# fc1's first half loaded in two parts around row 0 of x, chunks 0 and 1 computed row by row, and the second half's banks transposed behind each chunk's row 1

## The chip, the core and the metric

One core of a Trainium2 chip runs the kernel. TensorE (PE) multiplies and transposes, ScalarE (ACT), VectorE (DVE) and GpSimd (POOL) work on its results, and SyncE (SP) and ScalarE issue the transfers. The metric is the device time of one execution in microseconds (us).

## The reference

x is 32 rows of 256 tokens with 256 features, all float32. Each row has an index that picks one of 16 experts.

```python
h = gelu(einsum('bnd,hd->bnh', x, fc1_w) + fc1_b)        # fc1_w 1024 x 256, exact GELU
shared = einsum('bnh,sh->bns', h, fc2_w) + fc2_b         # fc2_w 192 x 1024
expert_x = einsum('bnh,bph->bnp', h, experts_w[indices]) + experts_b[indices][:, None, :]
out = x + concatenate([shared, expert_x], axis=-1)       # experts_w 16 x 64 x 1024
```

## The kernel before

The 32 rows of x are 16 blocks of R = 2 rows, 512 tokens each. A block's hidden features are K = 8 chunks of 128. Every float32 operand is split into a high part (rounded to the fast format, made by ScalarE with a copy) and a low part (the difference, made by VectorE or GpSimd), and a product is three matmuls: high-high, high-low, low-high. With D = 2 halves of the 256 features a chunk of fc1 is six matmuls of 512 columns. Blocks 0 and 1 are computed plainly (`conv_chunk`), the other 14 by a scheme with seven products in place of eight, whose weight sums are made while the first two blocks run. Every engine has its program written out by hand; the order of the lines is the order in its queue.

The change touches the first microseconds only.

- SyncE issues row 0 and row 1 of x (L318), waits for row 0 (L320), then issues fc1's second half (L321, in `load_w1`), the fc2 pieces, the experts of block 0 (after the index) and everything later. ScalarE issues the index (L615), fc1's first half (L617) and fc1's bias (L618).
- TensorE makes `WARM` = 12 matmuls on the identity (`warm`, L1052), transposes row 0 and row 1 of x into two banks of `tr_ps`, one bank for each half of the features (`x0_banks`, L1046), transposes fc1's first half from four strips (Q = 4) into the two banks of `acc_ps` (`w1_bank`, L1068), transposes the bias (L1206), computes chunk 0 (`first_chunk`, L1093), transposes fc1's second half into the banks of `tr_ps` once x's parts are made (L1209 to L1211), and goes on with `conv_chunk` 1 to 7 (L1086). Chunks 0 to 3 need only fc1's first half.
- ScalarE makes the high parts: `x0_high` (L461), `w1_high` of the first half (L474), then chunk 0's GELU (`conv_chunk` in its own program, L577), `w1_high` of the second half's two banks, chunk 1's GELU, and the fc2 high parts (`w2_high`, L484) between the next GELUs. `conv_high(0)` (`pair_high`, L565) follows the fourth of them.
- VectorE makes the low parts: `x0_low` (L708), `w1_low` (L721), then fc2's squares, which are 32x32 transposes into the banks of `acc_ps` (`w2_square`, L744), and their low parts (`w2_low`, L752). A square of a bank waits for the low part that frees it.
- GpSimd's first work after the identity is the low part of pair 0 of the hidden values (`pair_lo(0)`, L395), which waits for `conv_high(0)`.
- TensorE's first fc2 products (`fc2_first(0, 0, 8)`, L1222, matmuls at L1136) follow chunk 7 and wait for that low part. `conv_chunk(8)`, block 1's first chunk, waits for block 1's low part (`x1_low`, L813).

The order of the second half around chunks 0 and 1 is in ScalarE's program:

```python
conv_chunk(0)
w1_high(1, 0)
w1_high(1, 1)
conv_chunk(1)
w2_high(0)
```

Of the kernel before, what the change touches and what calls it, by code (L numbers as in the profile page):

```python
# [15 lines left out]
def cond_mlp_residual(nc, x, index, fc1_w, fc1_b, fc2_w, fc2_b, experts_w, experts_b, out):  # L16
# [17 lines left out]
    BANK = 512  # L34
    GELUS = 4
    SLOTS = 6
    WARM = 12

# [28 lines left out]
    with ctx:  # L67
# [6 lines left out]
        def sem(name):  # L74
            return ctx.enter_context(nc.semaphore(name))
# [46 lines left out]
        e_loaded = [sem(f"e_loaded{n}") for n in range(2)]  # L122
        be_loaded = [sem(f"be_loaded{n}") for n in range(2)]
        stored = [sem(f"stored{n}") for n in range(2)]
        w1_loaded = [sem(f"w1_loaded{n}") for n in range(2)]
        w1p_loaded = sem("w1p_loaded")
        w2_loaded = sem("w2_loaded")
        b1_loaded = sem("b1_loaded")
# [132 lines left out]
        def feature_chunk(rows, d):  # L261
            return rows.rearrange("p (c d) -> p d c", d=D)[:, d, :]
# [1 line left out]
        def bank(i):  # L264
            return fc1_ps[:, i, :].rearrange("p (j t) -> p j t", j=2)

        def load_w1(queue, half):
            queue.dma_start(w1_in[:, half * HALF:(half + 1) * HALF, :], w1_halves[half])\
                .then_inc(w1_loaded[half], 16)

        block = ctx.enter_context(nc.Block())

# [1 line left out]
        def _(sp):  # L274
# [41 lines left out]
            for b in range(R):  # L316
                ts = slice(b * T, (b + 1) * T)
                sp.dma_start(resid[:, 0, ts, :], x_blocks[0][:, ts, :]).then_inc(x0_loaded[b], 16)  # L318

            sp.wait_ge(x0_loaded[0], 16)  # L320
            load_w1(sp, 1)  # L321
            for q in range(Q):
                sp.dma_start(w2_piece[S * q:S * (q + 1), :, :], w2_v[q]).then_inc(w2_loaded, 16)
            sp.wait_ge(index_loaded, 16)
# [46 lines left out]
        def _(pool):  # L371
            def residual(n, b):
                par = n % 2
                if n == 0:
                    pool.wait_ge(x0_loaded[b], 16)

                    pool.wait_ge(x0_tr, D)
                else:
                    pool.wait_ge(x_loaded[par], 16 * ((n + 1) // 2))
                pool.wait_ge(b2_loaded, 16)  # L380
                pool.wait_ge(be_loaded[par], 16 * R * (n // 2 + 1))
                rows = resid[:, par, b * T:(b + 1) * T, :]
# [73 lines left out]

        @block.scalar
        def _(act):
            def x0_high(d):
                act.wait_ge(x0_tr, d + 1)  # L460
                nc.scalar.activation(xt0[:, d, HI, :], tr_ps[:, d, :], ACT.Copy)\  # L461
                    .then_inc(x0_hi, 1)

            def w1_slots(half, d, v):

# [130 lines left out]
            def lower_pair(t):  # L596
# [15 lines left out]
                act.wait_ge(c21_gelu, 2 * t + 2)  # L612
                pair_high(q)

            act.dma_start(index_sb[:, :], index.rearrange("(o n) -> o n", o=1))\  # L615
                .then_inc(index_loaded, 16)
            load_w1(act, 0)  # L617
            act.dma_start(b1_in[:, :].rearrange("k (q c) -> k q c", q=Q),  # L618
                          fc1_b.rearrange("(q k c) -> k q c", q=Q, c=S))\
                .then_inc(b1_loaded, 16)  # L620
# [2 lines left out]
            nc.scalar.activation(gelu[:, 0, 0, 0:1], ident[:, 0:1], ACT.Gelu)\  # L623
                .then_inc(gelu_loaded, 1)
            act.wait_ge(gelu_loaded, 1)
            for d in range(D):
                x0_high(d)
            for d in range(D):
                w1_high(0, d)
            act.wait_ge(b1_ready, 1)  # L630
            conv_chunk(0)
            w1_high(1, 0)
            w1_high(1, 1)
            conv_chunk(1)
            w2_high(0)
            w2_high(1)
            conv_chunk(2)
# [65 lines left out]

        @block.vector
        def _(dve):
            def x0_low(d):
                dve.wait_ge(x0_hi, d + 1)
                nc.vector.tensor_tensor(xt0[:, d, LO, :], tr_ps[:, d, :],  # L708
                                        xt0[:, d, HI, :].bitcast(FP32), ALU.subtract)\
                    .then_inc(x0_lo, 1)  # L710

            def w1_slots(half, d, v):
                cols = slice(2 * half * P, (2 * half + 2) * P)
# [215 lines left out]
                        else:  # L929
                            nc.vector.tensor_tensor(dst, src, dst, ALU.add).then_inc(drained, 1)  # L930

            for d in range(D):
                x0_low(d)
            for d in range(D):
                w1_low(0, d)
            dve.wait_ge(b1_tr, 1)
            nc.vector.tensor_copy(b1[:, :], fc1_ps[:, 3, 0:K]).then_inc(b1_ready, 1)
            for d in range(D):
# [104 lines left out]
        def _(pe):  # L1043
            def transposes(dst, tiles):
                for c, tile in enumerate(tiles):
                    last = nc.tensor.transpose(dst[:, c * P:(c + 1) * P], tile, ident[:, :])  # L1046
                return last
# [6 lines left out]

            def x0_banks(b):
                pe.wait_ge(x0_loaded[b], 16)
                for d in range(D):
                    last = transposes(tr_ps[:, d, b * SEQ:(b + 1) * SEQ],
                                      [feature_chunk(resid[:, 0, b * T + t, :], d)
                                       for t in range(T)])  # L1060
                    if b == R - 1:
                        last.then_inc(x0_tr, 1)

            def w1_bank(half, d):

                dst = (acc_ps, tr_ps)[half][:, d, :].rearrange("p (k q c) -> p q k c", q=Q, c=S)
                for q in range(Q):
                    last = nc.tensor.transpose(  # L1068
                        dst[:, q], feature_chunk(w1_in[:, half * HALF + q, :], d), ident[:, :])
                last.then_inc(w1_tr, 1)  # L1070

            def conv_operand(j, d, v):

# [14 lines left out]
                                            start=(at == 0), stop=(at == len(terms) - 1))  # L1088
                last.then_inc(conv_filled, 1)

            def first_chunk():
                def product(d, w, v):
                    return nc.tensor.matmul(fc1_ps[:, 0, :], conv_operand(0, d, w), xt0[:, d, v, :],  # L1093
                                            start=(d == 0 and w == v), stop=(d == D - 1 and w == LO))
                for d in range(D):
                    pe.wait_ge(w1_hi, d + 1)
                    product(d, HI, HI)
                    pe.wait_ge(x0_lo, d + 1)
                    product(d, HI, LO)
                for d in range(D):  # L1100
                    pe.wait_ge(w1_lo, d + 1)
                    last = product(d, LO, HI)
                last.then_inc(conv_filled, 1)

            def product(n, g, dst, w, o, fresh):

# [90 lines left out]

            pe.wait_ge(ident_ready, 1)
            warm(WARM)
            for b in range(R):  # L1200
                x0_banks(b)
            pe.wait_ge(w1_loaded[0], 16)
            for d in range(D):
                w1_bank(0, d)
            pe.wait_ge(b1_loaded, 16)
            nc.tensor.transpose(fc1_ps[:, 3, 0:K], b1_in[:, :], ident[0:K, 0:K]).then_inc(b1_tr, 1)  # L1206
            first_chunk()
            pe.wait_ge(w1_loaded[1], 16)
            for d in range(D):  # L1209
                pe.wait_ge(x0_lo, d + 1)  # L1210
                w1_bank(1, d)  # L1211
            conv_chunk(1)
            conv_chunk(2)
            conv_chunk(3)
            pe.wait_ge(w1_lo, 4)
# [102 lines left out]
```

## Time and profile before

| | |
|---|---|
| median of three executions | 357.48 us (357.47 to 357.76) |
| the profiled execution | 357.54 us, its span 355.4 us |
| busy in the span | TensorE 350.9 us, VectorE 259.5, ScalarE 246.8, GpSimd 235.0 |
| transferred | 28.68 MB read from memory, 8.39 MB written |

Times in the rows are us from the span's start. PE is TensorE's matmuls, PEld its weight loads, which run ahead of the matmuls. A row of the timeline merges instructions of one kind that follow each other: start, us, engine, line, operation, output and inputs, shape, count. In square brackets stands how long the engine sat idle before and what it waited for. The "us" of a merged row includes the tail of its last instruction, so that rows of TensorE overlap a little. In the chain of work that ended last the pieces don't overlap.

### The profile page before, as it was taken

The numbers are of one execution on the slowest core, as the hardware profiler recorded it, in microseconds if no ns is written. First come the engines' busy times: TensorE is split into PE (matmuls) and PEld (weight loads), VectorE is DVE, ScalarE is ACT, GpSimd is POOL, SyncE is SP. The second block draws the span as 40 slices with busy tenths as digits, with TensorE's granted clock in tenths as the row PEclk, the third lists the DMA queues.
The fourth block names the chain that finished last, engine by engine and source line by source line (L and its number), as shares of the span: only waits on it lengthen the run. The fifth ranks groups of instructions, "written<-read, shape, count | busy, mean of one in ns | idle before, by whom it ended". The sixth has DMA issues, their size and how long they took to land.

```text
span 355.4 us, 7075 instructions
## 1 busy us (share of the span) xinstructions
PE 350.9 (99%) x2381; PEld 323.7 (91%) x2381; DVE 259.5 (73%) x498; ACT 246.8 (69%) x410; POOL 235.0 (66%) x150
## 2 busy tenths in 40 slices
PE   8999999999999999999999999999999999999996
PEld 5899899999999999999999999999999999999996
DVE  2797976968859697786968869697786968844642
ACT  4885957777678577767777678577777777666560
POOL 0179887658866586865758866576865758855471
PEclk9999999999999999999999999999999999999999
DMA  8779663533333334341533324353332230312001
GB/s 239 172 162 191 140 181 85 148 99 89 112 87 117 89 90 141 94 110 59 149 98 89 114 79 122 90 137 101 84 107 64 90 99 30 120 38 89 31 30 61
DMA packets 69981, 37.53 MB, mean 106 GB/s; under 512 B 43450, under 2 KB 69946, under 8 KB 69946
## 3 DMA queue, kind: packets, MB, share of 16 engines
q1 hardware_dynamic: 69376, 36.55, 38.1%
q10 hardware_dynamic: 570, 0.53, 0.4%
q8 instruction: 19, 0.31, 0.4%
q14 instruction: 16, 0.13, 0.1%
HBM read 28.68 MB, written 8.39 MB: 104 GB/s over the span
## 4 chain that ended last, share of the span: by engine, by line
PE 98%; ACT 0%; issue 0%; POOL 0%; DVE 0%; POOLq 0%; ACTq 0%
PE fc_ps L1110 40%; PE acc_ps L1166 29%; PE acc_ps L1169 15%; PE fc_ps L1086 6%; PE acc_ps L1136 3%; PE acc_ps L1189 2%; PE fc_ps L1166 1%; PE fc_ps L1052 1%; PE fc_ps L1093 1%; PE fc_ps L1169 1%; PE tr_ps L1046 0%; ACT xt L461 0%; PE tr_ps L1068 0%; ACT w1t L474 0%; DVE resid L906 0%
## 5 line engine op out<-in xcount | busy, mean ns | idle before, releaser
L395 POOL TENSOR_TENSOR ht<-gelu,ht 128x1024 fp32r<-128x1024 f32 x62 | 149.5, 2411 | 97.4 <-ACT ht L565 97.4
L1166 PE MATMUL acc_ps<-w2t,ht 128*128 128x512 f32 x448 | 162.4, 397 | 0.0
L1110 PE MATMUL fc_ps<-xt,w1t 128*128 128x256 f32 x1176 | 159.9, 284 | 0.0
L1110 PEld LDWEIGHTS fc_ps<-xt,w1t 128*128 128x128 f32 x1176 | 148.7, 189 | 5.5
L1169 PE MATMUL acc_ps<-w2t,ht 128*128 128x256 f32 x448 | 125.9, 281 | 0.0
L1166 PEld LDWEIGHTS acc_ps<-w2t,ht 128*128 128x128 f32 x448 | 84.4, 188 | 14.9
L1169 PEld LDWEIGHTS acc_ps<-w2t,ht 128*128 128x128 f32 x448 | 85.0, 190 | 0.0
L565 ACT ACTIVATE ht<-gelu 128x1024 fp32r<-128x1024 f32 x64 | 68.0, 1063 | 3.6 <-issue 0.4
L591 ACT ACTIVATE gelu<-work,b 128x512 f32<-128x512 f32 x56 | 37.3, 715 | 26.2 <-DVE work L870 26.1
L403 POOL TENSOR_TENSOR xt<-work,xt 128x1024 fp32r<-128x1024 f32 x14 | 33.8, 2417 | 14.8 <-ACT xt L554 14.8
L870 DVE TENSOR_TENSOR work<-fc_ps,work 128x512 f32<-128x512 f32 x28 | 19.4, 692 | 22.6 <-PE fc_ps L1110 21.3
L863 DVE TENSOR_TENSOR work<-fc_ps,work 128x512 f32<-128x512 f32 x28 | 19.1, 681 | 20.6 <-PE fc_ps L1110 20.6
L383 POOL TENSOR_TENSOR resid<-resid,bias 128x384 f32<-128x384 f32 x32 | 33.9, 1061 | 0.0
L494 ACT ACTIVATE w2t<-tr_ps 128x512 fp32r<-128x512 f32 x28 | 16.8, 600 | 24.4 <-DVE tr_ps L763 24.4
L544 ACT ACTIVATE work<-fc_ps 128x512 f32<-128x512 f32 x28 | 16.8, 601 | 21.9 <-PE fc_ps L1110 21.8
L878 DVE TENSOR_TENSOR work<-fc_ps,work 128x512 f32<-128x512 f32 x28 | 19.4, 692 | 13.3 <-PE fc_ps L1110 13.3
L800 DVE TENSOR_TENSOR work<-b_rows 128x256 f32<-128x256 f32 x14 | 27.9, 1990 | 1.2 <-ACT b_rows L535 1.1
L930 DVE TENSOR_TENSOR resid<-acc_ps,resid 128x256 f32<-128x256 f32 x56 | 22.5, 422 | 7.3 <-PE acc_ps L1169 6.3
L603 ACT ACTIVATE gelu<-work,b 128x256 f32<-128x256 f32 x56 | 25.4, 508 | 0.0
L923 DVE TENSOR_TENSOR resid<-acc_ps,resid 128x192 f32<-128x192 f32 x56 | 19.9, 355 | 6.8 <-PE acc_ps L1169 5.8
L608 ACT ACTIVATE gelu<-fc_ps,b 128x256 f32<-128x256 f32 x56 | 23.5, 476 | 0.0
L1086 PE MATMUL fc_ps<-xt,w1t 128*128 128x512 f32 x90 | 22.0, 393 | 0.0
(73 smaller groups left out, 335.6 us busy)
## 6 DMA issues: line engine op xcount, KB each, us to landing
pieces<-in_L_cond_experts_w SPq DMA_DIRECT2D x128, 64.0 KB, 2.0
out<-resid SPq DMA_DIRECT2D x31, 256.0 KB, 3.1
pieces<-in_x SPq DMA_DIRECT2D x60, 128.0 KB, 2.9
resid<-in_x SPq DMA_DIRECT2D x15, 512.0 KB, 3.5
e_bias<-in_L_cond_experts_b SPq DMA_DIRECT2D x32, 32.0 KB, 2.8
work<-in_L_cond_fc_w SPq DMA_DIRECT2D x4, 256.0 KB, 4.7
w_piece<-in_L_cond_fc_w SPq DMA_DIRECT2D x4, 192.0 KB, 5.0
resid<-in_x SPq DMA_DIRECT2D x2, 256.0 KB, 3.2
```

What stands on the lines that cost most here:

```text
L383: nc.gpsimd.tensor_tensor(rows[:, :, 0:SHARED], rows[:, :, 0:SHARED], bias[:, :].unsqueeze(1).to_broadcast([P, T, SHARED]), ALU.add).then_ ...
L395: nc.gpsimd.tensor_tensor(ht[:, slot, LO, :, :].rearrange("p k t -> p (k t)"), gelu[:, q % GELUS, :, :].rearrange("p k t -> p (k t)"), ht[ ...
L403: nc.gpsimd.tensor_tensor(xt[:, n % 2, X_T1:X_T4 + 1, LO, :], t_sum, xt[:, n % 2, X_T1:X_T4 + 1, HI, :].bitcast(FP32), ALU.subtract).then_ ...
L565: nc.scalar.activation(ht[:, q % SLOTS, HI, :, :].rearrange("p k t -> p (k t)"), gelu[:, q % GELUS, :, :].rearrange("p k t -> p (k t)"), A ...
L591: nc.scalar.activation(gelu[:, q % GELUS, j, :], upper[:, j, :], ACT.Gelu, bias=b1[:, k:k + 1]).then_inc(up_gelu, 1)
L603: nc.scalar.activation(gelu[:, q % GELUS, j, SEQ:2 * SEQ], c22[:, j, :], ACT.Gelu, bias=b1[:, k:k + 1]).then_inc(c22_gelu, 1)
L608: nc.scalar.activation(gelu[:, q % GELUS, j, 0:SEQ], fc1_ps[:, BANK_A[t % 2], j * SEQ:(j + 1) * SEQ], ACT.Gelu, bias=b1[:, k:k + 1]).then_ ...
L800: nc.vector.tensor_tensor(t_sum[:, o, :], in0, in1, ALU.subtract)\
L1086: last = nc.tensor.matmul(fc1_ps[:, c % 4, :], conv_operand(k, d, w), xt_plain[c // K][:, d, v, :], start=(at == 0), stop=(at == len(terms ...
L1110: last = nc.tensor.matmul(fc1_ps[:, dst, j * SEQ:(j + 1) * SEQ], w1t[:, w, wv, ms], xt[:, n % 2, o, xv, :], start=(fresh and j == 0 and at ...
L1166: nc.tensor.matmul(acc.rearrange("p (v o) -> p v o", v=2), ht[:, q % SLOTS, HI, j, ts], w2t[:, :, k, fc2_columns(b)], start=(k == 0), stop ...
L1169: last = nc.tensor.matmul(acc[:, OUT:2 * OUT], ht[:, q % SLOTS, LO, j, ts], w2t[:, HI, k, fc2_columns(b)], start=False, stop=True, skip_gr ...
```

## The change

- fc1's first half is loaded in two transfers: strips 0 and 1 on ScalarE's queue ahead of the index, strips 2 and 3 on SyncE's queue between row 0 and row 1 of x. The second half's transfer is as before, with a semaphore of its own.
- `WARM` is 8.
- A bank of `tr_ps` now holds one row of x with both halves of its features, so that row 0's parts are made without row 1. ScalarE and VectorE make row 1's parts after the first half's.
- Chunks 0 and 1 are computed together, row by row (`first`): 24 matmuls of 256 columns in place of 12 of 512. Row 1 is transposed between row 0's first products.
- Each bank of the second half is transposed behind row 1 of a chunk (bank 0 behind chunk 0, bank 1 behind chunk 1) in place of both ahead of chunk 1. ScalarE copies bank 1 after chunk 1's GELU in place of before it.

```diff
-    WARM = 12
+    WARM = 8
...
+        def load_w1(queue, half, part, strips):
+            cols = slice(half * HALF + strips.start, half * HALF + strips.stop)
+            queue.dma_start(w1_in[:, cols, :], w1_halves[half][:, strips])\
+                .then_inc(w1_loaded[part], 16)
+
+        def x0_row(v, b):
+            return xt0[:, :, v, b * SEQ:(b + 1) * SEQ]
+
+        def x0_bank(b):
+            return tr_ps[:, b, :].rearrange("p (d t) -> p d t", d=D)
...
                 sp.dma_start(resid[:, 0, ts, :], x_blocks[0][:, ts, :]).then_inc(x0_loaded[b], 16)
+                if b == 0:
+                    load_w1(sp, 0, 1, slice(Q // 2, Q))
 
             sp.wait_ge(x0_loaded[0], 16)
-            load_w1(sp, 1)
+            load_w1(sp, 1, 2, slice(0, Q))
...
-                    pool.wait_ge(x0_tr, D)
+                    pool.wait_ge(x0_tr, R)
...
+            def x0_high(b):
+                act.wait_ge(x0_tr, b + 1)
+                nc.scalar.activation(x0_row(HI, b), x0_bank(b), ACT.Copy).then_inc(x0_hi, 1)
...
+            load_w1(act, 0, 0, slice(0, Q // 2))
             act.dma_start(index_sb[:, :], index.rearrange("(o n) -> o n", o=1))\
                 .then_inc(index_loaded, 16)
-            load_w1(act, 0)
...
-            for d in range(D):
-                x0_high(d)
+            x0_high(0)
             for d in range(D):
                 w1_high(0, d)
+            x0_high(1)
             act.wait_ge(b1_ready, 1)
             conv_chunk(0)
             w1_high(1, 0)
+            conv_chunk(1)
             w1_high(1, 1)
-            conv_chunk(1)
             w2_high(0)
...
-            for d in range(D):
-                x0_low(d)
+            x0_low(0)
             for d in range(D):
                 w1_low(0, d)
+            x0_low(1)
...
+                transposes(tr_ps[:, b, :], [feature_chunk(resid[:, 0, b * T + t, :], d)
+                                            for d in range(D) for t in range(T)]).then_inc(x0_tr, 1)
...
+            def first(c, b, d, w, v):
+
+                return nc.tensor.matmul(fc1_ps[:, c, b * SEQ:(b + 1) * SEQ], conv_operand(c, d, w),
+                                        xt0[:, d, v, b * SEQ:(b + 1) * SEQ],
+                                        start=(b == 0 and d == 0 and w == v), stop=True,
+                                        skip_group_check=True)
...
-            for b in range(R):
-                x0_banks(b)
+            x0_banks(0)
             pe.wait_ge(w1_loaded[0], 16)
             for d in range(D):
-                w1_bank(0, d)
+                w1_strips(0, d, range(Q // 2))
+            pe.wait_ge(w1_loaded[1], 16)
+            for d in range(D):
+                w1_strips(0, d, range(Q // 2, Q)).then_inc(w1_tr, 1)
+
+            pe.wait_ge(x0_hi, 1)
+            pe.wait_ge(w1_hi, 1)
+            for c in range(2):
+                first(c, 0, 0, HI, HI)
+            x0_banks(1)
+            pe.wait_ge(w1_hi, 2)
+            for c in range(2):
+                first(c, 0, 1, HI, HI)
+            pe.wait_ge(x0_lo, 1)
+            for d in range(D):
+                for c in range(2):
+                    first(c, 0, d, HI, LO)
+            for d in range(D):
+                pe.wait_ge(w1_lo, d + 1)
+                for c in range(2):
+                    first(c, 0, d, LO, HI)
             pe.wait_ge(b1_loaded, 16)
             nc.tensor.transpose(fc1_ps[:, 3, 0:K], b1_in[:, :], ident[0:K, 0:K]).then_inc(b1_tr, 1)
-            first_chunk()
-            pe.wait_ge(w1_loaded[1], 16)
-            for d in range(D):
-                pe.wait_ge(x0_lo, d + 1)
-                w1_bank(1, d)
-            conv_chunk(1)
+
+
+            pe.wait_ge(x0_hi, 2)
+            for c in range(2):
+                for w, v in ((HI, HI), (LO, HI), (HI, LO)):
+                    if v == LO:
+                        pe.wait_ge(x0_lo, 2)
+                    for d in range(D):
+                        last = first(c, 1, d, w, v)
+                last.then_inc(conv_filled, 1)
+                if c == 0:
+                    pe.wait_ge(w1_loaded[2], 16)
+                w1_strips(1, c, range(Q)).then_inc(w1_tr, 1)
             conv_chunk(2)
```

## Rows read from the trace of the kernel before

**Rows 1.** The page's part 4: share of the chain by engine.
```profile
PE 98%; ACT 0%; issue 0%; POOL 0%; DVE 0%; POOLq 0%; ACTq 0%
```

**Rows 2.** Timeline of the first 20 us: TensorE's matmuls.
```profile
1.53 2.74 PE L1052 MATMUL fc_ps<-ident 128*128 128x256 bf16 x12 [1.53 <-POOL ident L421]
...
4.07 1.56 PE L1046 MATMUL tr_ps<-ident,resid 128*128 128x128 f32 x8
...
5.76 1.23 PE L1068 MATMUL acc_ps<-ident,w_in 128*128 128x128 f32 x8
...
7.19 1.98 PE L1093 MATMUL fc_ps<-xt,w1t 128*128 128x512 f32 x6
...
9.01 1.11 PE L1068 MATMUL tr_ps<-ident,w_in 128*128 128x128 f32 x8
```

**Rows 3.** The same timeline: weight loads that waited.
```profile
5.75 1.03 PEld L1068 LDWEIGHTS acc_ps<-ident,w_in 128*128 128x128 f32 x8 [0.32 <-DMA w_in<-in_L_cond_fc_w]
...
8.66 0.19 PEld L1093 LDWEIGHTS fc_ps<-xt,w1t 128*128 128x128 f32 x1 [0.41 <-DVE w1t L721]
```

**Rows 4.** The chain in order of time: start, us, engine, output, line, count.
```profile
10.11 9.57 PE fc_ps L1086 x42
...
44.34 2.17 PE fc_ps L1110 x18
```

**Rows 5.** Timeline, landing times of L318, and stretches (last column GB/s).
```profile
3.51 0.37 SPq L268 DMA_DIRECT2D w_in<-in_L_cond_fc_w  x1
...
DMA to landing us min/median/max: 2.7/3.2/3.6
...
1.50:3.00 1.50, 1.47 (x7) 1.04 (x8) 0.00 (x0) 0.74 (x1) 0.00 (x0) 1.00 0.61 189
3.00:3.75 0.75, 0.75 (x5) 0.56 (x4) 0.00 (x0) 0.74 (x2) 0.00 (x0) 1.00 1.00 337
3.75:4.50 0.75, 0.75 (x6) 0.69 (x5) 0.00 (x0) 0.00 (x1) 0.00 (x0) 1.00 1.08 374
```

**Rows 6.** Line L1046: durations in ns, least, median and most.
```profile
L1046 PE MATMUL tr_ps<-ident,resid x8: 273/324/421, 4.1 to 5.3; 128*128 128x128 f32 x8
```

**Rows 7.** Timeline: ScalarE and VectorE up to the first fc2 square.
```profile
5.49 1.09 ACT L461 ACTIVATE xt<-tr_ps 128x512 fp32r<-128x512 f32 x2 [1.74 <-PE tr_ps L1046]
...
9.26 0.69 ACT L577 ACTIVATE gelu<-fc_ps,b 128x512 f32<-128x512 f32 x1 [1.64 <-PE fc_ps L1093]
...
9.85 1.08 ACT L474 ACTIVATE w1t<-tr_ps 128x512 fp32r<-128x512 f32 x2
...
10.47 1.29 DVE L721 TENSOR_TENSOR w1t<-tr_ps,w1t 128x512 fp32r<-128x512 f32 x2 [1.80 <-ACT w1t L474]
...
11.68 1.04 DVE L744 STREAM_TRANSPOSE acc_ps<-w_piece 128x384 f32<-128x384 f32 x2
```

**Rows 8.** Timeline: from the fc2 squares to GpSimd's first low part.
```profile
14.48 0.59 DVE L744 STREAM_TRANSPOSE acc_ps<-w_piece 128x384 f32<-128x384 f32 x1
...
15.11 0.49 ACT L484 ACTIVATE w2t<-acc_ps 128x384 fp32r<-128x384 f32 x1
15.50 1.05 ACT L565 ACTIVATE ht<-gelu 128x1024 fp32r<-128x1024 f32 x1
...
16.63 2.41 POOL L395 TENSOR_TENSOR ht<-gelu,ht 128x1024 fp32r<-128x1024 f32 x1 [15.16 <-ACT ht L565]
...
19.30 0.89 PEld L1136 LDWEIGHTS acc_ps<-w2t,ht 128*128 128x128 f32 x6
19.52 0.76 PE L1136 MATMUL acc_ps<-w2t,ht 128*128 128x256 f32 x5
```

**Rows 9.** Timeline from 18.5: block 1's low part and chunk 8.
```profile
20.73 1.29 DVE L813 TENSOR_TENSOR xt<-tr_ps,xt 128x512 fp32r<-128x512 f32 x2 [0.43 <-ACT xt L515]
...
22.27 0.31 PEld L1086 LDWEIGHTS fc_ps<-xt,w1t 128*128 128x128 f32 x2
22.39 0.40 PE L1086 MATMUL fc_ps<-xt,w1t 128*128 128x512 f32 x1
```

More of the change, by code:

```diff
@@ L124, in cond_mlp_residual @@
         stored = [sem(f"stored{n}") for n in range(2)]
-        w1_loaded = [sem(f"w1_loaded{n}") for n in range(2)]
+        w1_loaded = [sem(f"w1_loaded{n}") for n in range(3)]
         w1p_loaded = sem("w1p_loaded")
@@ L265, in bank @@
             return fc1_ps[:, i, :].rearrange("p (j t) -> p j t", j=2)
-        def load_w1(queue, half):
-            queue.dma_start(w1_in[:, half * HALF:(half + 1) * HALF, :], w1_halves[half])\
-                .then_inc(w1_loaded[half], 16)
+        def load_w1(queue, half, part, strips):
[6 more added lines that the diff above has]
+            return tr_ps[:, b, :].rearrange("p (d t) -> p d t", d=D)
         block = ctx.enter_context(nc.Block())
@@ L458, in _ @@
         def _(act):
[L459 to L462, printed above, removed]
+            def x0_high(b):
+                act.wait_ge(x0_tr, b + 1)
+                nc.scalar.activation(x0_row(HI, b), x0_bank(b), ACT.Copy).then_inc(x0_hi, 1)
             def w1_slots(half, d, v):
@@ L705, in _, with x0_low @@
         def _(dve):
[L706 to L710, printed above, removed]
+            def x0_low(b):
+                dve.wait_ge(x0_hi, b + 1)
+                nc.vector.tensor_tensor(x0_row(LO, b), x0_bank(b), x0_row(HI, b).bitcast(FP32),
+                                        ALU.subtract).then_inc(x0_lo, 1)
             def w1_slots(half, d, v):
@@ L1056, in x0_banks, with w1_strips @@
                 pe.wait_ge(x0_loaded[b], 16)
-                for d in range(D):
[L1058 to L1064, printed above, removed]
+                transposes(tr_ps[:, b, :], [feature_chunk(resid[:, 0, b * T + t, :], d)
+                                            for d in range(D) for t in range(T)]).then_inc(x0_tr, 1)
+            def w1_strips(half, d, strips):
                 dst = (acc_ps, tr_ps)[half][:, d, :].rearrange("p (k q c) -> p q k c", q=Q, c=S)
-                for q in range(Q):
+                for q in strips:
                     last = nc.tensor.transpose(
                         dst[:, q], feature_chunk(w1_in[:, half * HALF + q, :], d), ident[:, :])
-                last.then_inc(w1_tr, 1)
+                return last
             def conv_operand(j, d, v):
@@ L1089, in conv_chunk @@
                 last.then_inc(conv_filled, 1)
[L1091 to L1097, printed above, removed]
-                    pe.wait_ge(x0_lo, d + 1)
[L1099 to L1103, printed above, removed]
+            def first(c, b, d, w, v):
[3 more added lines that the diff above has]
+                                        skip_group_check=True)
             def product(n, g, dst, w, o, fresh):
@@ L1199, in _ @@
             warm(WARM)
-            for b in range(R):
-                x0_banks(b)
+            x0_banks(0)
             pe.wait_ge(w1_loaded[0], 16)
             for d in range(D):
-                w1_bank(0, d)
+                w1_strips(0, d, range(Q // 2))
[18 more added lines that the diff above has]
+                    first(c, 0, d, LO, HI)
             pe.wait_ge(b1_loaded, 16)
             nc.tensor.transpose(fc1_ps[:, 3, 0:K], b1_in[:, :], ident[0:K, 0:K]).then_inc(b1_tr, 1)
-            first_chunk()
-            pe.wait_ge(w1_loaded[1], 16)
-            for d in range(D):
-                pe.wait_ge(x0_lo, d + 1)
-                w1_bank(1, d)
-            conv_chunk(1)
+            pe.wait_ge(x0_hi, 2)
[9 more added lines that the diff above has]
+                w1_strips(1, c, range(Q)).then_inc(w1_tr, 1)
             conv_chunk(2)
```

## The prediction

> **What bounds the kernel now.** I read the chain that ended last first, then the timeline of TensorE over the first 20 us, then the waits of its weight loads. The chain [rows 1] is TensorE for 98% of the span: whatever moves the first microseconds moves the end only by what it does to TensorE's own sequence, and after 10.11 that sequence has no hole [rows 4]. So I ask two things: when does the sequence from chunk 2 on begin, and does any later TensorE wait become late because another engine is later.
>
> Before chunk 2 TensorE does [rows 2]: 12 warm-up matmuls from 1.53, 8 transposes of x from 4.07, 8 of fc1's first half from 5.76, chunk 0 from 7.19, 8 transposes of fc1's second half from 9.01, and from then on the chunks without a break. It is held by the first half's transfer until 5.75 and by VectorE's low part before 8.66 [rows 3]. Eight transposes take 1.11 with a tail of 0.28, so one costs 0.83/7 = 0.12 [rows 2, 6]; from the chain's pace a 256-column product costs 2.17/18 = 0.12 and a 512-column one 9.57/42 = 0.228 [rows 4]. Chunk 2 begins at 10.11 + 6 x 0.228 = 11.48 by the chain's marks. These lie 0.16 behind the starts in the timeline (the 42 products end at 19.68, the next start is 19.52 [rows 4, 8]), and I count by starts: 11.32.
>
> **The transfers.** Now row 0 of x is issued at 0.75 and landed 2.7 later, at 3.5, where SyncE goes on with L268; the first half of fc1 lands just before 5.75 [rows 3, 5]. The new order puts a quarter (0.26 MB) of fc1 on ACT's queue at 0.75, beside row 0, and the next quarter on SyncE's queue ahead of row 1. Bytes moved, from the GB/s rows [rows 5]: 0.28 MB by 3.00, 0.54 by 3.75, 0.82 by 4.50. So 0.26 MB is through at 2.9, 0.52 at 3.7, 0.79 at 4.4, and row 0 landed 0.5 to 0.6 after its bytes. If row 0 still goes first it lands at 3.5, if it shares evenly at 4.2; I take 3.85, the middle, since no row favours an end. The first quarter is in by 4.2, the second by 4.9, row 1 by 5.7. The second half of fc1, issued when row 0 is in, moves from 3.51 to about 3.9; the transposes from 9.01 on had no wait for it [rows 2, 3], and the first of them comes later now, so it stays covered. So do the fc2 pieces behind it on SyncE's queue: they are read first at 11.68 now [rows 7] and later in the new order. Moving the index load behind the first quarter delays it by one issue (0.37 in [rows 5]), and nobody needs it before SyncE has issued the fc2 pieces.
>
> The trace cannot tell how two queues divide the transfer engines here. The Trainium skill (DMA: Bandwidth & Descriptors, Queues, rings and completion order) says that an engine takes turns between the queues that have work. By that row 0 would land at the late end, 4.2, and the sum below would be 0.15 higher.
>
> **TensorE up to the first product.** Eight warm-ups instead of twelve: 12 took 4.07 - 1.53 = 2.54, so 0.212 each, and the last now ends its turn at 3.22. A 256-column matmul in 0.212 is the lower of the two clocks, 1.2 GHz; the transposes of row 0 still have durations of up to 421 ns, the later ones 273 [rows 6], so the clock rose in mid-transposes, around 4.7. The new wait for row 0 leaves TensorE idle from 3.22 to 3.9. Then four transposes at 0.212 (3.9 to 4.75), four for the first quarter at 0.12 (to 5.25), and the second quarter's, in by 4.9, from 5.25. The second of these completes bank 0: it ends at 5.25 + 0.12 + 0.28 = 5.65. ScalarE, which copies row 0 at 5.1 to 5.7 (0.60 each, 0.50 apart, [rows 7]), begins the weight copy 0.10 later at 5.75, ends at 6.35, and TensorE's first product starts 0.05 later: P = 6.4 against 7.19. Ends: with row 0 at 4.2 two of its transposes run at the upper clock and P = 6.55; with row 0 at 3.5 and the second quarter at 4.9 P = 6.05.
>
> **TensorE from P to chunk 2.** All at 0.12, plus 0.10 for the first product, whose weights can't be loaded ahead: 2 products to P + 0.34, 4 transposes of row 1 to 0.82, 2 products to 1.06, 4 high-low to 1.54, 4 low-high to 2.02, the bias transpose to 2.14, 6 products of chunk 0's row 1 to 2.86, 4 transposes to 3.34, 6 products to 4.06, 4 transposes to P + 4.54. The waits inside are met: the second weight copy ends at P + 0.43, VectorE's low parts of the weights at P + 0.67 and P + 1.28 (needed at 1.54 and 1.78), row 1's high part at P + 1.67 and low part at P + 2.39 (needed at 2.14 and 2.62). The 0.41 idle of [rows 3] is gone; 24 products of 256 columns cost 2.88 where 12 of 512 cost 2.74, so the split by rows costs 0.14. Chunk 2 starts at 10.94 against 11.32: TensorE is 0.38 ahead (0.73 to 0.23 over the range of P).
>
> **What that does to the other engines.** Here the edit in ScalarE's order counts. Before, both banks of the second half were transposed before chunk 1, copied from 9.85, and VectorE's low parts ran from 10.47, so that its first fc2 square started at 11.68 [rows 7]. Now the second bank is transposed behind chunk 1 and copied behind chunk 1's GELU. The last matmul of chunk 1 ends at P + 4.22, the GELU starts 0.10 later, the copy 0.59 later [rows 7] at P + 4.91, ends at P + 5.50, VectorE's low part starts at P + 5.54, and the first square, queued behind it, 0.60 later: P + 6.13 = 12.53. That is 0.85 later than 11.68, while TensorE is 0.38 earlier. Queued behind it is a chain with no slack [rows 8]: each fc2 square waits for the low part that frees its bank (the fourth starts at 14.48), ScalarE's fourth high part starts at 15.11 as that ends, then pair 0's high part at 15.50, which ends at 16.55, and GpSimd's low part at 16.63, which takes 2.41 and ends at 19.04. TensorE's first fc2 needs that: its weight load starts at 19.30, so the slack was 0.22 (0.04 being the signal's). With the chain 0.85 later it can start at 19.93, and its products 0.10 after that, 20.03, against 19.52: TensorE is 0.5 behind where it was 0.4 ahead, so it idles 0.9. The next step is as tight: chunk 8 needs VectorE's low part of block 1, which ended at 20.73 + 1.29 = 22.02, with TensorE's load at 22.27 and product at 22.39 [rows 9]. That part hangs on the same chain (by the order of the programs ScalarE makes its high part behind pair 0's and pair 1's), so it ends at 22.87, the load starts at 22.91 and the product at 23.01: 0.62 behind. From then on ScalarE, VectorE and GpSimd have their usual waits for TensorE, and nothing is given back. The sum: P + 6.13 - 11.68 - 0.23 = P - 5.78 = +0.62, from +0.27 (P 6.05) to +0.77 (P 6.55). The profiled execution took 357.54, 0.06 over the median of 357.48; against it 357.54 + 0.62 = **358.16**, and 358.1 against the median: slower by 0.17%.
>
> **Rivals.** (1) *The clock rises later.* The clock rose after TensorE had worked without a pause from 1.53 to about 4.7. The new kernel has a pause of 0.3 to 1.0 in there and four warm-ups fewer, and no row shows the rise with such a pause. If it comes near 7.0 instead, the eight weight transposes cost 0.21 instead of 0.12 each, P moves by about 0.65, and the result is 358.8; if it comes at 8 or later, the products from P on lose another 0.5 and more: 359.4 to 360. It decides from a delay on that adds 0.1, where the sum passes 0.2%. For it speaks the pause, against it that TensorE still works for 1.7 before the pause and from 3.9 to 5.7 after it. The Trainium skill (TensorE: Matmul & The Clock Gate, Part 1) has it that activity releases the clock and that the point of the rise differs by some 0.5 us between runs. By that a pause can only speak for this rival, and even in my own case P could move by 0.1 to 0.2 either way. (2) *The lead arrives.* If the chain to the first fc2 isn't as rigid as I read it, or the GELU and the last copy fall closer together, TensorE keeps its 0.38: 357.1 (356.8 to 357.3). Against it: in [rows 8] the starts at 15.11 and 16.63 follow an end within 0.1, and 15.50 is as early as ScalarE's queue allows. (3) *The quarters are no earlier.* With both queues competing from 0.75, the second quarter could land with the old half, at 5.7: P = 5.75 + 1.15 = 6.9, +1.1, 358.6. Against it the bytes: 0.79 MB were through at 4.4.
>
> **How the numbers follow.** My case 55%, rival 1 17%, rival 2 18%, rival 3 10%. About 0.2% (0.7 us) is what a measurement of this kernel can tell from no change. My case spans that bound at 358.2: 35 of its 55 points lie within, 20 above. Rival 2 gives 12 faster and 6 within, rivals 1 and 3 give 25 slower and 2 within. Faster 0.12, same 0.43, slower 0.45. The range goes from 357.0, which takes in the near half of rival 2, to 359.4, which takes in rival 3 and rival 1 up to its second price; my own case alone is 357.8 to 358.3.
>
> **What would show it.** The first product near 6.4, chunk 2 near 10.9, VectorE's first fc2 square near 12.5, GpSimd's first low part ending near 19.9, and a TensorE wait of about 0.9 for it, which doesn't exist now. Wrong if fc2's first load still starts without a wait before 19.3, if the last copy of fc1 isn't behind chunk 1's GELU, or if products near 5 to 8 us run at half pace.

## The result and the profile after

| kernel | median | executions | ratio to before, 95% interval |
|---|---|---|---|
| before | 357.48 us | 357.28 to 357.76 | |
| changed | 360.15 us | 359.56 to 360.40 | 1.0067 (1.0057 to 1.0077) |

The change costs 2.67 us, four times the 0.62 of the forecast, and the time lies outside its range. The profiled execution took 359.56, the lowest of the six, with a span of 357.4 against 355.4. So the trace accounts for 2.0 of the difference. The other five executions are up to 0.8 longer and were not traced, so the remaining 0.65 of the median has no cause shown.

The chain that ended last, in order of time (start, us, engine, output, line, count), answers to [rows 4]:

```profile
0.75 3.46 DMA resid<-in_x
...
4.25 1.13 PE tr_ps L1053 x4
5.38 1.29 PE acc_ps L1071 x6
...
6.69 0.61 ACT w1t L482
...
7.43 0.77 PE fc_ps L1096 x2
8.20 0.52 PE tr_ps L1053 x4
8.72 1.19 PE fc_ps L1096 x10
...
11.07 0.69 ACT gelu L585
11.76 0.49 ACT w1t L482
12.25 0.65 ACT gelu L585
12.90 0.49 ACT w1t L482
...
14.03 0.59 DVE acc_ps L751
...
17.95 0.96 ACT ht L573
...
18.98 2.41 POOL ht L404
...
21.44 2.66 PE acc_ps L1132 x20
```

Before, TensorE held this chain from 10.11 on. Now it leaves TensorE at 11.0, runs through both GELUs and both copies of fc1's second half (L482), through VectorE's squares (L751) and pair 0's high and low parts, and comes back to TensorE only at 21.44. That is the chain of [rows 8], moved: the first square is at 14.03 for 11.68, GpSimd ends at 21.39 for 19.04. From the square to that end it is 7.36 in both.

The weight loads that waited, in total us, times, longest:

```profile
PEld tr_ps L1053 <- DMA resid<-in_x: 1.3, 1, 1.3
PEld acc_ps L1132 <- POOL ht L404: 1.0, 1, 1.0
PEld fc_ps L1096 <- issue: 0.7, 1, 0.7
```

The second is the wait foreseen at 0.9. The weight loads waited 1.0; counted by the starts of the products, as the prediction counts, it is 0.82 (36 products from 12.41 at 0.228 end at 20.62, the first fc2 product starts at 21.44). Upstream of it is a surprise in the durations (ns, least, median, most) of the eight transposes of fc1's first half, of the changed kernel:

```profile
L1071 PE MATMUL acc_ps<-ident,w_in x8: 417/417/417, 5.2 to 6.7; 128*128 128x128 f32 x8
```

All are as long as the transposes at the lower clock of [rows 6], and they start 0.21 apart where I had 0.12. TensorE did not reach its upper level (2.4 GHz) before 8 us; before, it had it from about 4.7.

This is read from the pace and not from the profile's granted clock, which stands at 1.00 for the first microseconds of both kernels, slow stretches included (the 5.00:6.00 rows further down). The one trace here in which the granted clock falls to 0.50, under "The old transfers", has the same slow pace there, so the pace is taken for the level: 0.21 a transpose is 1.2 GHz, 0.12 is 2.4 GHz.

### The profile page after: what moved, and what is told of

The parts are those of the page before. It is cut to its first block, busy times and chain, and to the rows that moved or that the text cites. A ratio compares the mean times of both kernels' runs of the same rounds, so it can differ in the third digit from the quotient of the medians.

```text
span 357.4 us, 7092 instructions
## 1 busy us (share of the span) xinstructions
PE 351.4 (98%) x2389; PEld 324.4 (91%) x2389; DVE 259.8 (73%) x498; ACT 246.8 (69%) x410; POOL 235.1 (66%) x150
## 4 chain that ended last, share of the span: by engine, by line
PE 95%; ACT 2%; DMA 1%; POOL 1%; DVE 1%; issue 0%; DVEq 0%; ACTq 0%
PE fc_ps L1106 40%; PE acc_ps L1162 29%; PE acc_ps L1165 15%; PE acc_ps L1132 3%; PE fc_ps L1089 3%; PE acc_ps L1185 2%; PE fc_ps L1162 1%; DMA resid<-in_x 1%; PE fc_ps L1096 1%; POOL ht L404 1%; ACT gelu L585 1%; PE fc_ps L1165 1%; PE tr_ps L1053 0%; ACT w1t L482 0%; ACT w2t L492 0%; PE acc_ps L1071 0%
## 5 line engine op out<-in xcount | busy, mean ns | idle before, releaser
L1089 PE MATMUL fc_ps<-xt,w1t 128*128 128x512 f32 x84 | 20.8, 394 | 0.0
```

The lines of the kernel that those rows point to most:

```text
L1089: last = nc.tensor.matmul(fc1_ps[:, c % 4, :], conv_operand(k, d, w), xt_plain[c // K][:, d, v, :], start=(at == 0), stop=(at == len(terms ...
```

## Experiments

Medians are compared with the kernel before as executed beside them: 357.65 in the first group (12 and 8 warm-ups, both banks, the banks apart), 357.51 in the second (16 warm-ups, the old transfers, SyncE not waiting, pair 0 first), 357.59 in the third (the changed kernel once more, the last version). The brackets behind a median are the lowest and highest execution, those behind a ratio its 95% interval. Each kernel is one of the two, or one built before it here, with the edit shown.

### 12 warm-ups in the changed kernel

```diff
-    WARM = 8
+    WARM = 12
```

> The changed kernel with 12 warm-up matmuls in place of 8, nothing else. Theory (the clock): the pause before row 0 of x shrinks from 0.83 to about 0.1 us and TensorE reaches the upper clock near 4.7 us as in the kernel before, not at 8.2; then the eight transposes of fc1's first half go at 0.12 us each, the first product starts at 6.5 to 6.6 (7.43 in the changed kernel), chunk 2 at about 11.1, the first fc2 square at about 12.7, and a TensorE wait of 0.8 to 0.9 for GpSimd's low part stays: 358.2 to 358.4 us. Rival (the clock has no part, the new order itself costs the time): no gain, 359.5 to 360.3. Second rival (the clock is all of it): 357.3 or less.

Measured: 358.89 us (358.14 to 359.30), 1.0031 (1.0019 to 1.0042). That is 1.24 over the kernel before, so of 2.67 about 1.4 go with the four warm-ups; the rivals "no part" and "all of it" both fall. The changed kernel wasn't executed in this group, and its one execution in the third (358.95, next section) lies within the range of this one, so the 1.4 is no firmer than the difference of two groups. The durations are those of the upper clock:

```profile
L1071 PE MATMUL acc_ps<-ident,w_in x8: 281/283/354, 5.4 to 6.3; 128*128 128x128 f32 x8
```

The time is 0.5 above what I expected. In the profiled execution, which took about the median (358.90), row 0 of x landed only at 4.80, so that the first product started at 7.15 in spite of the better clock; the others weren't traced. From there the working of the prediction fits: the first square came at 13.42, 6.27 after the first product (6.13 forecast), and the weight loads of the first fc2 waited 1.0, as in the changed kernel.

### The changed kernel once more

> The changed kernel unaltered, one more execution with its trace. Theory (with 8 warm-ups and the pause before row 0 the clock comes late as a rule, not by chance): the upper clock again after 7 us, the transposes of fc1's first half 0.21 us apart, the first product near 7.4, the first fc2 square near 14.0, 359.5 to 360.4 us. Rival (the rise at 8.2 was an accident of that execution): near 5, first product near 6.6, 358.2 to 358.9.

Measured: 358.95 us. The transposes' rows, from the timeline:

```profile
4.05 1.13 PE L1053 MATMUL tr_ps<-ident,resid 128*128 128x128 f32 x4 [0.63 <-DMA resid<-in_x]
4.97 1.91 PE L1071 MATMUL acc_ps<-ident,w_in 128*128 128x128 f32 x8
7.24 0.48 PE L1096 MATMUL fc_ps<-xt,w1t 128*128 128x256 f32 x2 [0.35 <-ACT w1t L482]
```

Row 0 was in by 4.05, yet eight transposes took 1.91, the lower clock again, and it had risen by the products at 7.24. Late here means after the eight weight transposes. So the late rise is not an accident of one execution, but when it comes varies (by 7.24 here, not by 8 in the first trace). The time was 0.5 below my lower bound of 359.5: chunk 2 began at 11.89 here and at 12.41 in the first trace, of which 0.2 is row 0's earlier landing and 0.3 the earlier rise.

### 16 warm-ups in the changed kernel

```diff
-    WARM = 8
+    WARM = 16
```

> The changed kernel with 16 warm-up matmuls in place of 8, nothing else: the last ends near 4.9, past the landing of row 0 in every trace so far (3.96 to 4.80), so TensorE never pauses before the transposes. Theory (pause and count decide when the clock rises, the landing of row 0 varies from run to run): the clock rises by 5.0 in every run, the runs differ less than those with 12 (358.14 to 359.3), first product near 6.8, median 358.4 to 358.8. Rival (warm-ups only cost their own time beyond the landing): as with 12 or slower, 358.9 to 359.3, with the same spread.

Measured: 359.12 us (358.53 to 359.70), 1.0041 (1.0028 to 1.0054). The rival holds: the extra warm-ups ran past row 0's landing, the first product started at 7.36, and the spread did not shrink (1.17 between lowest and highest, 1.16 with 12). Row 0 was in at 4.0 and its first transpose started at 4.92: past the landing a warm-up costs its own time.

### 8 warm-ups in the kernel before

```diff
-    WARM = 12
+    WARM = 8
```

> The kernel before with 8 warm-up matmuls in place of 12, nothing else. TensorE then has a pause of about 0.3 us before row 0 of x (landed at 3.5) and one of about 0.4 before row 1 (4.84). Theory (a pause with fewer matmuls ahead of it delays the clock): the upper clock comes near 8.2 in place of 4.7, the transposes of the first half take 1.7 instead of 1.0 us, the first products run at half pace, 358.3 to 358.8 us. Rival (only the longer pause of 0.83 us does it): the clock rises near 4.7 and the time is 357.4 to 357.6.

Measured: 358.36 us (357.25 to 359.06), 1.0025 (1.0011 to 1.0039).

```profile
L1068 PE MATMUL acc_ps<-ident,w_in x8: 421/421/487, 5.8 to 7.4; 128*128 128x128 f32 x8
```

With nothing else changed the four warm-ups cost 0.7 by the medians, the cleanest price of them here, since both kernels stood in one group. The profiled execution is one of the shorter (357.97): its first product is 0.69 later, chunk 2 and the first square 0.52, the end 0.43. One execution in eight took 357.25, within 0.05 of the kernel before at its best, so here too the rise is probably not late every time; it wasn't traced.

Whether the pause does it or the smaller number of matmuls ahead of it wasn't separated by an experiment, but the traces speak against the pause alone. TensorE paused 0.57 behind the 12 warm-ups of the first experiment and had the upper clock in the transposes right after. It paused 0.24 here and 0.63 in the second trace of the changed kernel, both times behind 8, and had it late. One trace further down has it late behind 12 with hardly a pause.

### Both banks of the second half ahead of chunk 1

With 12 warm-ups:

```diff
                 if c == 0:
                     pe.wait_ge(w1_loaded[2], 16)
-                w1_strips(1, c, range(Q)).then_inc(w1_tr, 1)
+                    for d in range(D):
+                        w1_strips(1, d, range(Q)).then_inc(w1_tr, 1)
...
-            conv_chunk(1)
             w1_high(1, 1)
+            conv_chunk(1)
```

> As the changed kernel with 12 warm-ups, but both banks of fc1's second half are transposed behind chunk 0 (before chunk 1's row 1) and both copied before chunk 1's GELU, as in the kernel before. Theory (the chain through the second bank): the last copy starts at about 10.7, the first fc2 square at about 12.0 in place of 12.7, GpSimd's first low part ends near 19.3, TensorE's wait for it nearly vanishes, 357.4 to 357.7 us. Rival (the place of the bank costs nothing): the same as with 12 warm-ups alone, about 358.3.

Measured: 358.13 us (357.71 to 358.64), 1.0015 (1.0006 to 1.0025): 0.76 less than with the banks apart, which refutes the rival, but 0.4 above what I expected, and the wait did not nearly vanish. In its profiled execution (357.71, the shortest of its ten) both copies stand together ahead of chunk 1's GELU. From its chain in order of time:

```profile
5.91 6.31 DMA w_piece<-in_L_cond_fc_w
...
12.24 0.60 DVE acc_ps L751
```

And from its waits, the loads of the first fc2:

```profile
PEld acc_ps L1132 <- POOL ht L404: 0.6, 1, 0.6
```

The square moved from 13.42 to 12.24, not to 12.0. VectorE's low parts started at 10.90, and by [rows 7] a square can start 1.21 after them, at 12.11; the last 0.13 is the fc2 pieces, which landed at 12.22. This trace is also the one to hold against the two of the changed kernel. Its row 0 was in at 3.96, its transposes of the first half took 1.25, and its first product was at 6.38, where I had put it:

```profile
4.07 0.69 PE L1053 MATMUL tr_ps<-ident,resid 128*128 128x128 f32 x4
4.60 1.25 PE L1071 MATMUL acc_ps<-ident,w_in 128*128 128x128 f32 x8
6.38 0.48 PE L1096 MATMUL fc_ps<-xt,w1t 128*128 128x256 f32 x2 [0.54 <-ACT w1t L482]
```

The second trace of the changed kernel had row 0 at 4.01 and its first product at 7.24: the lower clock is worth 0.86 at that point, about 0.4 in the transposes of row 0 and the rest in those of the first half.

### The banks apart in the kernel before

```diff
-            for d in range(D):
-                pe.wait_ge(x0_lo, d + 1)
-                w1_bank(1, d)
+            pe.wait_ge(x0_lo, 2)
+            w1_bank(1, 0)
             conv_chunk(1)
+            w1_bank(1, 1)
...
-            w1_high(1, 1)
             conv_chunk(1)
+            w1_high(1, 1)
```

> The kernel before with one part of the change: bank 0 of fc1's second half is transposed before chunk 1 and bank 1 behind it, and ScalarE copies bank 1 behind chunk 1's GELU. Theory (a rigid chain from the last copy to GpSimd's first low part): the copy starts near 11.7 (10.33 before), the first fc2 square near 12.9 (11.68), the first low part of GpSimd ends near 20.3 (19.05), and TensorE waits about 1.0 for it: 358.3 to 358.6 us. Rival (the chain has slack, or ScalarE and VectorE catch up): 357.4 to 357.7.

Measured: 358.66 us (358.27 to 359.09), 1.0032 (1.0022 to 1.0042), 1.0 more, at the upper end of what was expected. Timeline rows, of an execution that took 358.27, the shortest of its nine:

```profile
12.78 1.04 DVE L744 STREAM_TRANSPOSE acc_ps<-w_piece 128x384 f32<-128x384 f32 x2
...
17.73 2.39 POOL L395 TENSOR_TENSOR ht<-gelu,ht 128x1024 fp32r<-128x1024 f32 x1 [16.25 <-ACT ht L565]
...
20.18 1.01 PEld L1136 LDWEIGHTS acc_ps<-w2t,ht 128*128 128x128 f32 x8 [1.01 <-POOL ht L395]
```

The square is 1.10 later than in [rows 7], GpSimd's low part 1.10 later than in [rows 8], and a wait of 1.01 stands before the first fc2, where there was none. TensorE does the same instructions in another order, and chunk 2 starts at 11.14, some 0.2 earlier than before: a lead of 0.2 with a lag of 1.1 on the others costs 1.0. These two kernels have the same transfers and warm-ups and differ in the place of the second bank, so the pair shows this cause apart from the clock and the transfers.

### The old transfers

The kernel with both banks first and 12 warm-ups, with fc1's first half in one transfer behind the index:

```diff
-                if b == 0:
-                    load_w1(sp, 0, 1, slice(Q // 2, Q))
...
-            load_w1(act, 0, 0, slice(0, Q // 2))
             act.dma_start(index_sb[:, :], index.rearrange("(o n) -> o n", o=1))\
                 .then_inc(index_loaded, 16)
+            load_w1(act, 0, 0, slice(0, Q))
...
-            pe.wait_ge(w1_loaded[1], 16)
```

> 12 warm-ups and both banks of fc1's second half ahead of chunk 1, as before, and now also the transfers of the kernel before: fc1's first half in one transfer on ScalarE's queue behind the index, row 0 and row 1 of x on SyncE's. What is left of the change is the computing row by row. Theory (the new transfers cost: row 0 lands later beside the first quarter, SyncE therefore issues fc1's second half and the fc2 pieces later, and VectorE's first square waits for them at 12.2): row 0 lands at 3.5, the fc2 pieces at 11.1, the first product starts at about 7.1, the first square at about 12.3 because of the later product, 358.0 to 358.3 us. Rival (the transfers were worth their gain of 0.7 in the first product only): 358.5 to 358.9. Second rival: only the fc2 pieces counted: 357.4 to 357.7.

Measured: 360.31 us (359.07 to 360.58), 1.0059 (1.0037 to 1.0081); all three cases fall. Timeline rows, of the longest of its four executions:

```profile
6.26 1.22 PE L1069 MATMUL acc_ps<-ident,w_in 128*128 128x128 f32 x8 [1.38 <-DMA w_in<-in_L_cond_fc_w]
...
8.03 0.77 PE L1094 MATMUL fc_ps<-xt,w1t 128*128 128x256 f32 x2 [0.54 <-ACT w1t L480]
```

And the stretch in which the products begin, and a longer one from there (the last three figures are granted clock, transfer share and GB/s):

```profile
7.90:8.20 0.30, 0.17 (x1) 0.20 (x2) 0.29 (x1) 0.30 (x1) 0.00 (x0) 0.50 1.09 205
7.90:11.30 3.40, 3.27 (x15) 3.31 (x16) 1.98 (x3) 1.07 (x2) 0.00 (x0) 0.50 1.13 226
```

With row 1's transposes moved behind the first products, nothing covers the wait for the one transfer, which also landed 0.5 later than in [rows 3]. TensorE idled 1.38 and then 0.54, and the granted clock fell back to 0.50, the lower level, just as the products began. From the first product to chunk 2 it then took 6.17, against 4.73 with the new transfers. So this kernel doesn't price the transfers. Against the trace with both banks first, 1.65 of its lateness is there at the first product, and 1.44 is added behind it at the lower clock.

### SyncE not waiting for row 0

```diff
-            sp.wait_ge(x0_loaded[0], 16)
             load_w1(sp, 1, 2, slice(0, Q))
```

> 12 warm-ups, both banks ahead of chunk 1, the new transfers, and SyncE no longer waits for row 0 of x before it issues fc1's second half and the fc2 pieces. Theory (with both banks first, the fc2 pieces' landing at 12.2 sets VectorE's first square, which stood ready at 12.1): the pieces land at 11.4 to 11.8, the square moves only to 12.1 where VectorE comes free, 358.0 us, a gain of 0.1 at most; only if row 0 of x isn't disturbed. Rival (the queue was the bound of the whole chain): 357.5.

Measured: 358.32 us (357.81 to 358.58), 1.0018 (1.0009 to 1.0028), no gain over 358.13; the rival falls. The stretch from 5 to 6 us (last column GB/s), of the kernel before, the changed one and this one:

```profile
5.00:6.00 1.00, 0.87 (x6) 0.68 (x7) 0.00 (x0) 0.51 (x2) 0.00 (x0) 1.00 1.04 310
```

```profile
5.00:6.00 1.00, 1.00 (x6) 1.00 (x5) 0.00 (x0) 0.52 (x1) 0.00 (x0) 1.00 0.50 99
```

```profile
5.00:6.00 1.00, 1.00 (x9) 0.90 (x7) 0.21 (x1) 0.68 (x2) 0.00 (x0) 1.00 0.99 291
```

My reading, which no run isolates: before, the rest of fc1's first half on ScalarE's queue moved while SyncE's queue waited for its next data; the change took it out of there and left a hole. Issuing earlier closed most of the hole, but the fc2 pieces were no earlier (12.2), and what sets their landing then stays open. The square, at 12.39, doesn't test them: row 0 of x landed at 4.28, the first product came at 6.66, VectorE's low parts started at 11.18, and the square followed 1.21 later, as in [rows 7]. So the condition set above, that row 0 isn't disturbed, was not met.

### Pair 0's high part ahead of the fc2 high parts

The kernel with both banks first, with ScalarE's order changed:

```diff
             conv_chunk(1)
+            conv_high(0)
             w2_high(0)
             w2_high(1)
             conv_chunk(2)
             w2_high(2)
             conv_chunk(3)
             w2_high(3)
-            conv_high(0)
```

> 12 warm-ups, both banks ahead of chunk 1, and ScalarE makes pair 0's high part directly behind chunk 1's GELU, ahead of the four fc2 high parts, so that GpSimd's low part no longer hangs on the fc2 squares. Theory (TensorE's wait at the first fc2 is the chain through pair 0's high part; the next one, through block 1's low part, is as tight): GpSimd starts near 13.1 in place of 17.2, the wait of 0.6 before the first fc2 goes, and a wait of 0.1 to 0.4 before chunk 8 or the first fc2's expert weights takes its place: 357.6 to 358.0 us. Rival (that chain alone held TensorE): 357.3 or less. Second rival (nothing gained, the lateness only moves): 358.1.

Measured: 358.17 us (357.94 to 358.71), 1.0016 (1.0006 to 1.0025): the second rival, nothing gained.

```profile
14.20 2.41 POOL L404 TENSOR_TENSOR ht<-gelu,ht 128x1024 fp32r<-128x1024 f32 x1 [12.72 <-ACT ht L573]
...
20.32 3.03 PE L1132 MATMUL acc_ps<-w2t,ht 128*128 128x256 f32 x24
...
23.72 0.30 PEld L1089 LDWEIGHTS fc_ps<-xt,w1t 128*128 128x128 f32 x2 [0.57 <-DVE xt L820]
```

GpSimd was done at 16.61, and the first fc2 had no wait at all. The same 0.6 now stands before chunk 8, for block 1's low part (L820), the step of [rows 9]. From the start of VectorE's low parts of fc1's second half to the end of that part it is 11.68 with both banks first and 11.74 here (11.92 to 23.66): ScalarE and VectorE have the same amount to do in between, and putting pair 0 first only chooses where TensorE waits. This profiled execution was the longest of its ten and had the lower clock until past 6.5 in spite of 12 warm-ups, so 12 don't guarantee the early rise.

### A version built on this

From the kernel before, with its transfers, warm-ups and 512-column products; the waits for low parts are filled with chunk 1's products, the low-high products of both chunks follow, and the second half is transposed and copied earlier instead of later:

```diff
                 for d in range(D):
                     pe.wait_ge(w1_hi, d + 1)
-                    product(d, HI, HI)
+                    for c in range(2):
+                        product(c, d, HI, HI)
                     pe.wait_ge(x0_lo, d + 1)
-                    product(d, HI, LO)
+                    for c in range(2):
+                        product(c, d, HI, LO)
+                    if d == 0:
+                        pe.wait_ge(w1_loaded[1], 16)
+                        pe.wait_ge(x0_lo, D)
+                        for bank_d in range(D):
+                            w1_bank(1, bank_d)
...
-            act.wait_ge(b1_ready, 1)
-            conv_chunk(0)
             w1_high(1, 0)
             w1_high(1, 1)
+            act.wait_ge(b1_ready, 1)
+            conv_chunk(0)
             conv_chunk(1)
```

> A version built on the findings, from the kernel before: 12 warm-ups, its transfers, 512-column products, but chunks 0 and 1 interleaved so that their high-high and high-low products fill the waits for the low parts, and both banks of fc1's second half transposed after the first four products, copied ahead of chunk 0's GELU. Theory (a lead of TensorE counts only if the chain over the last copy, the squares, pair 0 and block 1 leads too): chunk 2 at 11.0 (11.34 before), VectorE's first square at 11.1 to 11.3 (11.69 before, bounded by the landing of the fc2 pieces), no wait at the first fc2, 357.1 to 357.3 us against 357.5. Rival (ScalarE, where chunk 0's GELU is now later, holds pair 0's high part back): 357.5 to 357.8 with a wait at the first fc2.

Measured: 357.35 us (357.08 to 358.15), 0.9991 (0.9982 to 1.0000). It is 0.24 below the kernel before, which the interval, touching 1, just fails to tell from no change, and 2.9 below the changed kernel when each is held against its own neighbours. The profiled execution was the slowest of the eleven, and its rows show the exposure:

```profile
6.41 1.23 PE L1068 MATMUL acc_ps<-ident,w_in 128*128 128x128 f32 x8 [0.75 <-DMA w_in<-in_L_cond_fc_w]
...
12.27 1.05 DVE L744 STREAM_TRANSPOSE acc_ps<-w_piece 128x384 f32<-128x384 f32 x2 [0.43 <-DMA w_piece<-in_L_cond_fc_w]
```

The first half landed 0.65 later than in [rows 3] and the fc2 pieces at 12.24, and still no load of the first fc2 waited. An execution with the usual landings was not traced, so that chunk 2 started at 11.0 in the others is inferred from their times.

## Why the prediction was wrong

**Right: the chain through the second bank.** The step "What that does to the other engines" stands. In the kernel before alone, the banks apart cost 1.0, with the square 1.10 later and a new wait of 1.01; in the changed kernel with 12 warm-ups, putting them together gave 0.76 back. The stretch from the first square to GpSimd's end was 7.34 to 7.37 in every trace but the two with another order on ScalarE. "Nothing is given back" held too, and early pair 0 showed that block 1's low part is as tight as I read it.

**Failed: "the clock rose in mid-transposes, around 4.7".** I carried that moment over to a kernel with four warm-ups fewer and a pause, and gave its being late 17%. In both traces of the changed kernel, and in that of the kernel before with 8 warm-ups, the transposes of the first half ran at the lower clock throughout. The price at the first product was 0.67 in the first trace (7.43 against the forecast 6.4, less 0.36 for row 0's landing); the rival had 0.65 there. It came out at 358.8, or 359.4 and more with a rise after 8: the mechanism was named and rightly priced, its chance was too small. The rule of the Trainium skill beside it (TensorE: Matmul & The Clock Gate, Part 1), that activity releases the clock and that the point varies by some 0.5 us, agrees in kind: the changed kernel's clock had risen by 7.24 in one trace and not yet by 8 in the other. The spread was wider than 0.5: behind 12 warm-ups the slow pace was over by 5 in most traces and lasted past 6.5 in one. Its seven executions differ by 1.45 us, those of the kernel before beside the first six by 0.48.

**Failed: the terms were kept apart.** I treated late transfers and a late clock as alternatives. They add. Row 0 landed at 4.2 in the first trace (4.01 in the second, 4.8 with 12 warm-ups, 3.96 with both banks first), where I took 3.85 from the middle. The rule of the Trainium skill on taking turns (DMA: Bandwidth & Descriptors, Queues, rings and completion order) gave 4.2: the first trace lies there, the others on both sides of it. The first product came at 7.43 instead of 6.4: 0.36 from row 0, the other 0.67 from the clock. By the prediction's own formula P - 5.78 this is +1.65; the trace has +2.0.

**The rest of the 2.0.** Chunk 2 came at P + 4.98 and the square at P + 6.60 (4.54 and 6.13 forecast). With the upper clock (12 warm-ups) it was 4.66 and 6.27, so 0.1 of it is a mis-sized term, the bias transpose between products: I had 0.12 for it, which would put the products on its two sides 0.24 apart, and they were 0.36 apart. The other 0.3 is the lower clock, which still held after the first product.

**Failed without harm: "so do the fc2 pieces", covered.** They landed at 11.96 in the changed kernel. There VectorE was later still, so nothing waited; once the banks were put together the square stood behind them for 0.13.

**What stays open.** With 12 warm-ups and the banks together 0.5 us remain over the kernel before. The profiled one, at 357.71 the shortest of its ten and so 0.4 below their median, had TensorE 0.2 ahead at chunk 2 and the chain 0.56 behind at the square, which is the forecast's picture at a smaller size; it accounts for 0.2 of the 0.5. Which share of it is the transfers' and which the row-by-row order's could not be told, since the order without the new transfers ran into a pause of its own. Open too are the 0.65 by which the changed kernel's median lies above its traced execution, and what makes the clock rise late behind 8 warm-ups.

## What to carry to other kernels

A kernel bound by one engine still has a fixed pipeline on the others behind its first results. Before moving a step behind others to let the bound engine start earlier, follow that step's output to the next wait of the bound engine: with the banks apart in the kernel before, the lead was 0.2 and the lag 1.1, and only the lag counted. Warm-up work is priced by what the clock does afterwards, not by its own length. A start with less of it, or with a pause, is a risk that no trace of the fuller start can bound, so it deserves its full price in the range, on top of late transfers.

## What the hardware showed

- The moment at which TensorE's clock reaches the upper level is not fixed by the kernel (read from the pace, it had risen by 7.24 in one execution of the changed one and after 8 in another). With 8 warm-ups and a pause after them the eight transposes of the first half ran at the lower clock in three traces of three; with 12 or more they ran at the upper one in eight of nine.
- The clock can fall back: after TensorE had idled 1.38 and then 0.54 us, the granted clock was at 0.50 when the products came, and stayed there for 3.4 us.
- A transfer came later beside another one issued at the same time on a second queue: row 0 of x landed at 3.96 to 4.80 beside a transfer on ScalarE's queue, and at 3.4 to 3.6 with that transfer issued 0.55 later.
- Landings vary by up to a us with the same issue order: fc1's first half 5.7 to 6.4, the fc2 pieces 11.1 to 12.2, in the five traces that have the transfers of the kernel before, three of them at the early end.
